# A graph network kernel on one core: the queries of every second tile gathered by index, and the untouched rows dealt out anew over three stages

## What is computed

```python
h = relu(layernorm(x))
x = x + relu(segment_sum(w_e * (h @ W)[src], dst))        # layer 0
h = relu(layernorm(x))
Q, K, V = h @ Wq, h @ Wk, h @ Wv                          # 8 heads of 32
score = (Q[dst] * K[src]).sum(per head) / sqrt(32)
score = score + relu(efeat @ W1 + b1) @ W2 + b2
alpha = softmax of score over the edges with the same dst
x = x + segment_sum(alpha * V[src], dst) @ Wo + bo        # layer 1
```

## Time and profile before

| | |
|---|---|
| median of 3 runs | 818.31 us (816.94 to 819.22) |
| profiled execution | 815.25 us, span 813.1 us |
| busy in the span | PE 694.8 us (85%), DVE 580.4 (71%), POOL 506.1 (62%), ACT 467.7 (58%) |
| DMA | 224.01 MB, mean 276 GB/s |
| mean granted TensorE clock | 0.963 of full speed |

### The profile page before, as it was taken

One profiled execution on the slowest core, in us unless ns is written; L12 is line 12 of the kernel. 1 busy time (PEld: TensorE's weight loads), 2 busy tenths in 40 slices (PEclk: granted clock), 3 DMA queues, 4 the chain that ended last, 5 costly groups with the idle time before them and its releaser, 6 DMA issues.

```text
span 813.1 us, 13370 instructions
## 1 busy us (share of the span) xinstructions
PE 694.8 (85%) x3804; PEld 546.8 (67%) x3804; DVE 580.4 (71%) x1676; ACT 467.7 (58%) x1383; POOL 506.1 (62%) x429
## 2 busy tenths in 40 slices
PE   1578999999799899962999999999998759999990
PEld 0346666666566667742878888888887637777770
DVE  5598888888877676700587565566567859999990
ACT  1557888887588789750444444444446276777700
POOL 6788887788878865206767576566402005777773
PEclk9989999999999999995999999999999978999996
DMA  6688999999989999696479799799796995766751
GB/s 176 212 272 261 335 326 338 354 356 334 321 246 340 312 341 357 231 358 202 151 258 329 275 362 355 283 328 374 253 351 187 269 316 168 222 202 215 231 170 52
DMA packets 122581, 224.01 MB, mean 276 GB/s; under 512 B 27475, under 2 KB 100828, under 8 KB 112142
## 3 DMA queue, kind: packets, MB, share of 16 engines
q1 hardware_dynamic: 74238, 150.45, 54.1%
q0 software_dynamic: 20464, 45.19, 18.6%
q10 hardware_dynamic: 27808, 27.53, 9.7%
HBM read 133.06 MB, written 102.76 MB: 290 GB/s over the span
## 4 chain that ended last, share of the span: by engine, by line
PE 49%; DVE 19%; DMA 15%; ACT 6%; issue 5%; POOL 3%; ACTq 1%; SPq 0%; DVEq 0%; POOLq 0%
PE bank L1018 43%; DVE small L1002 9%; DMA q<-ringC 5%; PE bank L1128 3%; DMA ringB<-x 2%; ACT ringB L623 2%; DVE small L801 2%; DVE store L991 2%; DMA work<-in_x 2%; PE bank L1109 2%; POOL out_x L522 2%; DMA ringA<-in_x,first_src 2%; DVE ringA L982 2%; PE bank L1084 1%; DMA out_x<-work 1%
## 5 line engine op out<-in xcount | busy, mean ns | idle before, releaser
L472 POOL DMA_INDIRECT store<-h,slot_gather x98 | 141.0, 1439 | 107.5 <-PE bank L1128 53.4
L1018 PE MATMUL bank<-Wkv_sb,small 128*128 128x256 f32 x784 | 186.6, 381 | 1.7 <-issue 1.7
L1018 PEld LDWEIGHTS bank<-Wkv_sb,small 128*128 128x128 f32 x784 | 149.9, 191 | 22.8 <-issue 2.1
L522 POOL DMA_INDIRECT out_x<-store,out_scatter x98 | 97.2, 991 | 52.5 <-issue 42.7
L472 POOL DMA_INDIRECT ringC<-in_x,dst_gather x98 | 92.7, 946 | 40.9 <-issue 25.6
L891 DVE TENSOR_TENSOR work<-bank,msgs 128x256 f32<-128x256 f32 x98 | 41.3, 422 | 107.6 <-PE bank L1018 107.6
L651 ACT COPY store<-bank 128x256 f32<-128x256 f32 x98 | 36.5, 372 | 134.3 <-PE bank L1018 134.3
L1018 PE MATMUL bank<-Wo_sb,small 128*128 128x256 f32 x392 | 109.7, 404 | 4.4 <-DVE small L1002 4.4
L679 ACT ACTIVATE ringA<-store,scores 128x32 f32<-128x32 f32 x392 | 87.6, 307 | 33.4 <-PE bank L1196 29.5
L1018 PE MATMUL bank<-W_sb,small 128*128 128x256 f32 x392 | 104.0, 389 | 0.0
L1018 PE MATMUL bank<-Wq_sb,small 128*128 128x256 f32 x392 | 101.5, 382 | 1.7 <-ACT ringC L555 1.6
(11 more groups left out here) (184 smaller groups left out, 1271.0 us busy)
## 6 DMA issues: line engine op xcount, KB each, us to landing
out_x<-bulk SPq DMA_DIRECT2D x33, 1152.0 KB, 7.6
bulk<-in_x SPq DMA_DIRECT2D x30, 1152.0 KB, 9.7
ringA<-q SPq DMA_DIRECT2D x14, 896.0 KB, 10.3
ringB<-x SPq DMA_DIRECT2D x12, 896.0 KB, 5.6
out_x<-ringC SPq DMA_DIRECT2D x9, 1152.0 KB, 6.5
ringC<-in_x SPq DMA_DIRECT2D x8, 1152.0 KB
x<-ringB SPq DMA_DIRECT2D x14, 512.0 KB, 5.9
h<-ringB ACTq DMA_DIRECT2D x14, 512.0 KB, 5.3
```

Of the source, the lines that this page charges most:

```text
L472: pool.indirect_dma_start(to, None, table, bass.IndirectOffsetOnAxis(ap=at, axis=0), **more).then_inc(landed, 16)
L522: pool.indirect_dma_start(out, bass.IndirectOffsetOnAxis(ap=out_i[:, t:t + 1], axis=0), store[:, t * D:(t + 1) * D], None, bounds_check=N ...
L1018: return nc.tensor.matmul(o, lhsT, rhs, start=start, stop=stop)
```

## The change

- Tiles 0 to 13 and every odd tile after them (56 of 98) take q by a gather of its own: POOL fetches for each edge the q row of its run's end (`qg_i`, made from `w_last` by a transpose on PE) straight into `ringA`, four tiles behind the gather of h2. These tiles have no spread on PE and no copy of it on ACT; DVE multiplies from `ringA`.
- The 42 even tiles from 14 on (`spread(t)`) keep the product with `same`. `q_in` loads only their pieces (4 or 3 per group, groups 2 to 13), in two transfers: 127 rows from `q_d`, and row 127 from a small table `q_open_rows`. The writes of `q_open` into `q_d` and the extra read are gone.
- Bulk units: 12 instead of 14 in the edges stage, 27 instead of 24 up to the middle's end (two of them right at its start), 5 instead of 6 in the softmax.

```diff
-EARLY = G
+EARLY = G - 2
-MIDDLE = EARLY + 24
+MIDDLE = EARLY + 27
...
+        def spread(t):
+            return t >= 2 * J and t % 2 == 0
+        def spreads(t):
+            return max(0, (t - 2 * J + 1) // 2)
...
             def q_in(a):
-                sp.dma_start(group(ringA, a % 2), edge_rows(q_d, a)).then_inc(ql[a % 2], 16)
+                rows_in = group(ringA, a % 2)[:, a % 2::2, :]
+                sp.dma_start(rows_in[0:P - 1], edge_rows(q_d, a)[0:P - 1, a % 2::2, :]).then_inc(ql[a % 2], 16)
+                sp.dma_start(rows_in[P - 1:P], open_d[J * a + a % 2:J * (a + 1):2, :][None, :, :]).then_inc(ql[a % 2], 16)
...
-            bulk_load(EARLY)
-            bulk_load(EARLY + 1)
-            sp.wait_ge(h1, T)
+            for u in range(EARLY, EARLY + 2):
+                bulk_load(u)
+            for u in range(EARLY, EARLY + 2):
+                bulk_store(u)
             for i in range(2):
-                sp.wait_ge(st_q[i], 32)
-            for a in range(2):
-                q_in(a)
-            for a in range(2):
-                sp.wait_ge(ql[a], 16)
+                sp.wait_ge(st_q[i], 16 * G)
+            for u in range(EARLY + 2, EARLY + 4):
+                bulk_load(u)
             sp.wait_ge(open_in, 16)
-            sp.dma_start(q_d.rearrange("(t p) d -> t p d", p=P)[:, P - 1, :], q_open).then_inc(open_out, 16)
-            sp.wait_ge(open_out, 16)
-            sp.dma_start(ringA[P - 1:P, :].rearrange("o (u d) -> o u d", d=D),
-                         q_d.rearrange("(t p) d -> p t d", p=P)[P - 1:P, 0:2 * J, :]).then_inc(open_to, 16)
-            bulk_load(EARLY + 2)
+            sp.dma_start(open_d, q_open).then_inc(open_out, 16)
...
                 if g + 2 < G:
-                    sp.wait_ge(same_rdy, g + 1)
-                    ends_in(g + 2)
-                    sp.wait_ge(qs, J * (g + 1))
+                    if g == 0:
+                        sp.wait_ge(open_out, 16)
+                    if g >= 2:
+                        sp.wait_ge(same_rdy, g - 1)
+                        ends_in(g + 2)
+                        sp.wait_ge(qs, spreads(J * (g + 1)))
+                    else:
+                        sp.wait_ge(k3, J * (g + 1))
                     q_in(g + 2)
...
-            for t in range(T):
-                if t == 4:
+            lead = 4
+            for t in range(T + lead):
+                if t < T:
+                    need(pool, t3, t - 2 * J + 1)
+                    fetch(store[:, t * D:(t + 1) * D], h2_d, slot_i[:, t:t + 1], o_in[t % (2 * J)],
+                          bounds_check=EP - 1, oob_is_err=False)
+                v = t - lead
+                if v == 0:
                     for i in range(2):
                         pool.wait_ge(st_q[i], 16 * G)
+                    pool.wait_ge(h1, T)
+                    pool.wait_ge(s_qg, 1)
+                if v >= 0 and not spread(v):
+                    need(pool, k3, v - 2 * J + 1)
+                    fetch(A(v % (2 * J)), q_d, qg_i[:, q_at(v):q_at(v) + 1], x_in[v % (2 * J)])
+                if v == 5:
                     fetch(q_open, q_d, end_i[:, 0:1], open_in)
...
-                        dve.wait_ge(qc, t + 1)
-                        nc.vector.tensor_tensor(prod[:, j, :], bank[6 + t % 2][:, 0:D], msg(t), ALU.mult).then_inc(k3, 1)
+                        if spread(t):
+                            q_rows = msg(spreads(t))
+                            dve.wait_ge(qc, spreads(t) + 1)
+                        else:
+                            q_rows = A(t % (2 * J))
+                            dve.wait_ge(x_in[t % (2 * J)], q_landed(t))
+                        nc.vector.tensor_tensor(prod[:, j, :], bank[6 + t % 2][:, 0:D], q_rows, ALU.mult).then_inc(k3, 1)
```

More of the change, by code:

```diff
@@ L273, in units, with q_at, q_landed @@
         def units(g):
-            k = MIDDLE - EARLY
-            return range(EARLY + k * g // G, EARLY + k * (g + 1) // G)
+            k = MIDDLE - EARLY - 2
+            return range(EARLY + 2 + k * g // G, EARLY + 2 + k * (g + 1) // G)
+        def spread(t):
+            return t >= 2 * J and t % 2 == 0
+        def spreads(t):
+            return max(0, (t - 2 * J + 1) // 2)
+        def q_at(t):
+            return t if t < 2 * J else J + t // 2
+        def q_landed(t):
+            return 16 * (T // (2 * J) + t // (2 * J) + 1)
         HAD = [EARLY // 2 + (MIDDLE - EARLY) // 3] * 2 + [(MIDDLE - EARLY) // 3, 0]
@@ L646, in _ @@
                 if t > 0:
-                    act.wait_ge(qs, t)
-                    need(act, k3, t - 2)
-                    nc.scalar.copy(msg(t - 1), bank[(t - 1) % 2][:, 0:D]).then_inc(qc, 1)
+                    if spread(t - 1):
+                        n = spreads(t - 1)
+                        act.wait_ge(qs, n + 1)
+                        need(act, k3, t - 4 if n > 1 else 0)
+                        nc.scalar.copy(msg(n), bank[n % 2][:, 0:D]).then_inc(qc, 1)
                     act.wait_ge(kv, t)
@@ L785, in slots @@
                     ins.then_inc(keys_rd, 1)
+                if g == -1:
+                    dve.wait_ge(s_tr, 8)
+                    nc.vector.tensor_copy(qg_i[:, 0:2 * J], bank[4][:, 2 * P:2 * P + 2 * J])
+                    nc.vector.tensor_copy(qg_i[:, 2 * J:], bank[4][:, 2 * P + 2 * J + 1:2 * P + T:2]).then_inc(s_qg, 1)
                 for j in range(J):
@@ L847, in same_run @@
             def same_run(a):
-                dve.wait_ge(end_in[a % 2], 16 * (a // 2 + 1))
-                need(dve, qs, J * (a - 1))
+                dve.wait_ge(end_in[a % 2], 16 * (a // 2))
+                need(dve, qs, spreads(J * (a - 1)))
                 nc.vector.tensor_scalar(same[a % 2], run_ends[a % 2], row_no[:, :], None, ALU.is_equal).then_inc(same_rdy, 1)
@@ L884, in pairs @@
                 if g == 0:
-                    same_run(0)
+                    for u in range(EARLY, EARLY + 2):
+                        add_unit(u)
                 for j in range(J + 1):
@@ L1132, in _ @@
                     v = t - 1
[L1133 to L1138, removed]
+                    if spread(v):
+                        a, n = v // J, spreads(v)
+                        if v < J * a + 2:
+                            pe.wait_ge(same_rdy, a - 1)
+                            pe.wait_ge(ql[a % 2], 32 * (a // 2))
+                        need(pe, qc, n - 1)
+                        mm(bank[n % 2][:, 0:D], same[a % 2][:, v % J * P:(v % J + 1) * P], A(v % (2 * J))).then_inc(qs, 1)
                     pe.wait_ge(hT3, v + 1)
```

19 lines of the change are left out of this document (10 added, 9 removed).

## The result

The changed kernel takes **989.03 us** (median of four executions, 980.89 to 993.17), the kernel before, run beside it on the same chip, 817.62 us (810.67 to 819.22). The ratio is **1.2104** (95% interval 1.1999 to 1.2209): slower by 171 us. The forecast was 1034 us in 905 to 1125.

What follows compares the result with a forecast made beforehand. PE was taken to bound the middle stage. From 815.25 us, plus 226 for q's loads on one DMA engine, less 10 in the softmax, came 1031 us; the median 3 over it, 1034 us, range 905 to 1125.

Steps and rivals of the forecast that it cites:

- One engine, always the same: Middle stage: every 127-row load of q goes to the same DMA engine, +226 us, 1034 us in all; chance 0.80.
- the rival of another engine each time: Middle stage: each load of q uses one DMA engine, but another each time, +125 us, 933 us in all; chance 0.05.
- PE relieved: Middle stage: PE loses 56 spreads of 0.43 us, 24 us, and 9 us of waiting at the start.
- rival 1: Middle stage: the 127-row load is spread over many engines, POOL sets the stage, 816 us (805 to 826); chance 0.13.
- the step on POOL: Middle stage: 155 gathers, 200 us, and 25 additions hitting them, 55 us, end POOL's work at 623 us, used by 627 to 628.
- The start: Middle stage: group 0 takes no `q_in`; that of group 2 comes at 398 us and lands at 429 us.
- The price of q on one engine: Middle stage: 47 ns per piece, 5.97 us per tile, 251 us for the 42 tiles together.
- What else that engine carries: Middle stage: the loaded engine's sixteenth of all other traffic, 15.6 us per group (13.5 to 18).
- Where it is waited for: Middle stage, SP's in-order queue: stores behind `q_in` wait on the loaded engine; lead hides 33 us, not 19 us every group.
- The rule of rival 1 for k engines: Middle stage: loads of q cost 251 / k us; with the other 217 us, under POOL's 255 us from k = 7 on.
- The softmax: Between last scores and POOL's scatter: five bulk units, a smaller last one, 10 us off (0 to 14).
- What was to show it: Profile signs: q load landing after 25 us or more, group windows 33 to 38 us, DMA share about one half, scatter 126 us.

Runs made afterwards that it cites:

- x1: The changed kernel with the 127 rows of each load of q split into transfers of 112 and 15 rows: 813.1 us, 0.9976 against before.
- x4: The changed kernel with the 127 rows of each load of q split into 116 and 11 rows: 821.4 us.
- x2: The changed kernel with the 127 rows of each load of q split into 41, 43 and 43 rows, all prime: 987.5 us.
- x5: x1 with q gathered after tile 13 only for the first two tiles of each group of seven, 38 gathers instead of 56: 808.4 us, 0.9917 against before.
- x6: x5 with q gathered after tile 13 only for the first tile of each group, 26 gathers: 807.1 us, 0.9890 against before.
- x7: x5 with q gathered after tile 13 for no tile, 14 gathers: 813.6 us, 0.9975 against before.
- x9: The changed kernel with the one-row transfer of q put ahead of the 127-row one: 993.6 us.
- x8: The kernel before with only the bulk units dealt out as 12, 27 and 5: 807.3 us, 0.9857 against before.
- x11: x5 with DVE adding bo to only one ninth of each of the middle stage's 25 bulk units: 799.4 us, 0.9799 against before.
- x3: The changed kernel with the 127 rows of each load of q split into 118 and 9 rows: 872.3 us.

## Why the prediction was right, and where its sizes were off

**Direction and cause: right.** One engine, always the same, was the forecast; the counts of x1 to x4 show the dealing, the share of 6.4% the one engine at work, x2 the same engine. The size is 45 us too high: the stated range of 905 to 1125 us holds 989, the narrower one for this case alone, 990 to 1120, just doesn't. The page of the Trainium skill that the prediction cited, "DMA: Bandwidth & Descriptors", section "Why a DMA increments its semaphore by 16 and not by 1", agrees with all five counts and with x2. It was also right against the rival of another engine each time, by 56 us.

**PE relieved, and POOL instead: right in the sum.** With the load spread, rival 1 gave 816 us and x1 took 813.1; POOL works from one gather straight to the next, and the stage is 257 us long where the step on POOL has 620.3 + 8 - 368.4 = 260. That PE alone would have been 33 us quicker isn't shown: in x5, x6 and x7 fewer spreads made the stage no shorter, and the first 14 tiles, where the prediction counted a gain of 9 us for PE, cost 7. The 8 us "more than PE's 33" were 6.

**The start: right.** `q_in` of group 2 was put at 398 us, 29.6 us after POOL's first gather, and landing at 429, 60.6 after it. It was issued at 391.38 and complete at 427.41, which is 29.2 and 65.2 us. Its 36 us to landing are five more than the 31 forecast; that pieces of the first units were still ahead of it is likely, not shown.

**The price of q on one engine: nearly right.** Four pieces and three differ by 5.7 us, which is 45 ns per piece and 5.7 us per tile, against 5.97 (47 ns). Over 38 tiles that is 10 us less.

**What else the engine carries: the term that was mis-sized.** From 427.41 us to 775.65, where PE takes up the last group, are 348.2 us for eleven groups. With 38 x 5.7 = 216.6 us for q, 131.6 are left, **12.0 us per group, not 15.6**: 40 us less, and below the lower bound of 13.5. The stage was to last 847 - 368.4 = 479 us and lasted 431, 48 less: the 50, and 2 at the tail after the last landing (17.6 us instead of 20), less the 5 that the first landing came later.

**Where it is waited for: right in effect, incomplete in kind.** The prediction had SP waiting for stores whose share lies on the loaded engine. That wait is there (7 us before the unit's load at 622.46), but the larger one is SP's own: it is held 20 to 29 us at issuing. Whether the stores' pieces would alone have made the same period isn't separated; x9 shows only that the order of the two loads of q doesn't matter.

**The rule of rival 1 for k engines: right in form.** 251 / k + 217 gives 468, 342 and 280 us for one, two and four engines; 431, 314 and 275 were measured. The first two are off by the term above (37 and 28 us), the third by 5 only: with four engines the loads of q come more slowly than the engine's work explains (x4). POOL was to set the stage from seven engines on: four are too few, as forecast, and between four and sixteen nothing was run.

**The softmax: right.** 10 us forecast, 8.9 measured in the changed kernel, and 7 to 12 in every other.

**The bulk units.** The two fewer in the edges stage were costed at nothing, and the stage's start shows no gain beyond its own spread (360 to 375 us in the kernels with 12 such units, 368 before). The three more in the middle were priced only as traffic on the loaded engine; where the engines are evenly loaded they cost nothing that shows (x8, 250.8 us against 251.6), and so the softmax's share is all the gain that there is in the change.

**What was to show it.** The first load landed after 36 us (25 or more; the profile gives no landing for the others), the groups took 23 to 37 us by PE's starts, 31.7 on average, seven of eleven less than the 33 to 38 forecast, as the term above has it, the scatter took 126 us as before (840.3 to 966.8), the DMA share was 0.51 (one half), a large load has one packet more than its pieces, and PE and POOL idled. Only the name of PE's wait was another: the page gives "issue" for all gaps but the first.

## What to carry to other kernels

Before a transfer whose number of rows 16 doesn't divide goes into a loop, count what it is dealt to: here the counts of small closing packets told it for every split tried, and 127 rows as 112 + 15 cost one more instruction and gave back 176 us. An engine's relief is worth what the next engine leaves of it, and the stage's first tiles count as much as its steady part: 38 gathers took 10 us of work from PE and cost it 12 us of idleness, 7 us of the stage in the first 14 tiles. When a change has several parts, time each alone; here the part that looked like housekeeping, the dealing of the bulk units, carried all the gain.

## What was not expected of the hardware

- With a transfer of 381 to 508 pieces on one DMA engine, the engine that issues is held too: SP stood 19.7 to 28.7 us at the next transfer, be it a load of four pieces or, in x9, a store (10 to 21 us, where it came 5 to 14 us later), and was free again before the loads had landed (420.3 against 427.4 us for the first).
- The mean busy share of the DMA engines can read 1.01 (x8) and doesn't stop the work: PE was busy 100 of 100 us beneath it in x8, and 183.1 of 186 beneath 0.97 in x11. Taken as a sum of what must be carried it was too high here (15.6 us a group against 12.0).
- The start of the stage moves by over 10 us between executions of programs that are the same up to there (360.06 us in x4, 372.09 in x3, 374.53 in x9), which is as much as most of what was measured here. Lengths of stages told the kernels apart where times of day did not.
